# Attention's routing parts of VectorE placed by a table of steps

## The chip, the cores and the metric

One core of one Trainium2 chip runs the whole program as one launch. The metric is the device time of that launch in microseconds (us). A profiled execution of the kernel before comes with its trace.

## What is computed

The input is x, 32 batches of 256 tokens of width 256, with a context of the same shape and a mask of 256x256 for each batch. The reference, cut to what matters:

```python
x = x + cross_attention(layernorm(x), ctx, ctx, mask, Wq, Wk, Wv, Wo, heads=16)   # head width 64
t = layernorm(x)
scores = sigmoid(t @ gate_w.T)                     # 16 experts
_, idx = top_k(scores + gate_b, 4)
w = take(scores, idx); w = w / sum(w) * 2.5
y = sum over the 4 chosen experts e of w_e * (silu_and_mul(t @ w13_e.T) @ w2_e.T)
out = x + y + silu_and_mul(t @ w13_s.T) @ w2_s.T   # one shared expert
```

## The kernel before, in words

The program has two phases. Attention (`emit_attention`) does the 32 batches one after another, 16 heads each, and writes x plus attention to memory; beside it, it already does the routing for the mixture of experts. The expert phase (`expert_phase`) then runs sorted tiles of tokens through the experts. This text is about the attention phase.

**Steps.** A step g is one head: g = 16 b + h, with batch b and h from 0 to 15, 512 steps in all, and a few more at the end. Every engine has its own loop over the steps, written out by hand, and the engines meet by semaphores. In a step TensorE does the scores of head g into `pS` (L888, L889), one projection for a later head into `pj` (a K part in even steps, a Q part in odd ones, L85 to L87, the first "fill"), the transposes of step g-3 into `pT` (L899), in most steps a second fill of `pj` (V at h = 4, 5, 12, 13; a part of Wo at h = 14, 0, 6, 8; transposes at h = 9 and 2; the logits at h = 7), and the values of step g-4 into `pV` (L912). `pj` is two banks: a fill waits until VectorE has emptied the bank of the fill before the last (`bank`, which waits for `s_pjfree`).

**VectorE's step** is, in this order: the masked scores of head g with their maximum, which writes `E` (L1130, two instructions), the inverse sums (L1105), the sum of the two heads' values (L1140), the low part of the first fill (`qk_sp`, L1097), the low part of the transposed probabilities (`PT_lo`, L1149), the low part or sum of the second fill (V L1093, L1078, L1085, L1088), now and then a part of a layer norm (statistics at h = 0, 2, 10, 11; aggregates at h = 4, 12; the norm at h = 6, 8), and last the routing's parts. GpSimd scales `E` by the inverse sums (L792), forms `att_lo` (L741) in even steps, splits the next context at h = 3 (L734, L736), and scatters rows to the experts' order by indirect DMAs (L771).

**Routing.** Two things are done on VectorE in small parts, each part at the end of a step.

- A *choice* (`Router.choose`, part k) takes a set of two batches: sigmoid, bias, the four best of 16 experts, their one-hot rows, their sum as a mask, and the weights. Set s starts at step `SET_FROM[s]` + 1, which is h = 9 of an odd batch, and does one part in each of 15 steps: 0 to 6 at h = 9 to 15, 7 to 14 at h = 0 to 7 of the even batch that follows. Part 11 has two instructions, a product of one-hot rows and scores into `r_prod` (L253) and a sum over it (L256). There are 15 such sets in this phase; a sixteenth is done in the expert phase.
- The *places* (`Router.place`) are computed for two groups of batches, after TensorE has counted ranks (`ranks`) at steps 266 and 426 (h = 10 of batches 16 and 26). Parts 0 to 7 are small. Then come 7 pieces (5 for the second group), each a product into `r_prod` (L327) and a sum (L331), and three parts of `row_of_place`. Before the change they took 18 (16) steps in a row, 267 to 284 and 427 to 442.

The scatters of a group, 8 for a batch and one every 1.5 steps, begin on GpSimd one step after the last part of its places (`scatter_at`), and each batch's rows are loaded again 8 steps before its first scatter (`reload_at`, SP's queue).

Of the kernel before, what the change touches and what calls it, by code (L numbers as in the profile page):

```python
# [41 lines left out]
EARLY_GROUPS = 2  # L42
# [3 lines left out]
SET_BATCHES = 2  # L46
SET_TILES = SET_BATCHES * BATCH_TILES
SETS = GROUP_START[-1] // SET_BATCHES
# [115 lines left out]
class Router:  # L164
# [49 lines left out]
        sc = self.sc[s % 2]  # L214
        act.activation(sc[:, :, :], sc[:, :, :], ACT.Exp, scale=-1.0).then_inc(self.s_exp, 1)

    SET_STEPS = 15

    def choose(self, dve, s, k):
        sc = self.sc[s % 2]  # L220
        at = slice(self.region(SET_TILES * s), self.region(SET_TILES * s) + SET_TILES)
        onehot = self.onehot[:, at, :, :]
        if k == 0:
            dve.wait_ge(self.s_exp, s + 1)
            self.chain(dve.tensor_scalar(sc[:, :, :], sc[:, :, :], 1.0, None, ALU.add))
            return
        self.chain_here(dve)
        if k == 1:
            self.chain(dve.reciprocal(sc[:, :, :], sc[:, :, :]))
        elif k == 2:  # L230
            self.chain(dve.tensor_tensor(self.bi[:, :, :], sc[:, :, :],
                                         self.shared.gate_b[:, :].unsqueeze(1).broadcast_to([P, SET_TILES, N_EXPERTS]), ALU.add))
        elif k in (3, 4):
            for t in range(2 * (k - 3), 2 * (k - 2)):
                last = dve.max(self.top[:, t, :], self.bi[:, t, :])
            self.chain(last)
        elif k in (5, 6):
            for t in range(2 * (k - 5), 2 * (k - 4)):
                last = dve.max_index(self.topi[:, t, :], self.top[:, t, :], self.bi[:, t, :])
            self.chain(last)  # L240
        elif k == 7:
            self.chain(dve.tensor_copy(self.topf[:, :, :], self.topi[:, :, 0:TOPK]))
        elif k == 8:
            self.chain(dve.tensor_tensor(
                onehot, self.shared.iota[:, :].unsqueeze(1).unsqueeze(1).broadcast_to([P, SET_TILES, TOPK, N_EXPERTS]),
                self.topf[:, :, :].unsqueeze(3).broadcast_to([P, SET_TILES, TOPK, N_EXPERTS]), ALU.is_equal))
        elif k == 9:
            self.chain(dve.tensor_tensor(self.halves[:, :, :, :], onehot[:, :, 0:2, :], onehot[:, :, 2:4, :], ALU.add))
        elif k == 10:
            dve.tensor_tensor(self.mask[:, at, :], self.halves[:, :, 0, :], self.halves[:, :, 1, :], ALU.add).then_inc(  # L250
                self.s_mask, 1)
        elif k == 11:
            self.chain(dve.tensor_tensor(self.prod[:, :, :, :], onehot,  # L253
                                         sc[:, :, :].unsqueeze(2).broadcast_to([P, SET_TILES, TOPK, N_EXPERTS]), ALU.mult))
            self.chain_here(dve)
            self.chain(dve.reduce_sum(self.taken[:, :, :], self.prod[:, :, :, :], AXX))  # L256
        elif k == 12:
            self.chain(dve.reduce_sum(self.wsum[:, :], self.taken[:, :, :], AXX))
        elif k == 13:
            self.chain(dve.reciprocal(self.wrec[:, :], self.wsum[:, :]))  # L260
        else:
            dve.scalar_tensor_tensor(self.shared.weight[:, SET_TILES * s:SET_TILES * (s + 1), :], self.taken[:, :, :], ROUTE_SCALE,
                                     self.wrec[:, :].unsqueeze(2).broadcast_to([P, SET_TILES, TOPK]), ALU.mult,
                                     ALU.mult).then_inc(self.s_weight, 1)
# [99 lines left out]
def emit_attention(nc, shared, ident_dram, gate_wT, gate_b, iota, x, ctxT, mask, wqT, wkT, wvT, woT, x2, w13_sT, w2_sT, w13T, w2T):  # L364
# [3 lines left out]
    H = INNER // DH  # L368
# [23 lines left out]
    router = shared.router  # L392
    SET_FROM = [(SET_BATCHES * s + SET_BATCHES + 1) * H + LG_STEP + 1 for s in range(SETS - 1)]
    RANK_STEP = 10
    RANKS_AT = [(GROUP_START[g + 1] + 2) * H + RANK_STEP for g in range(EARLY_GROUPS)]
    SCATTER_STEPS = 1.5
    scatter_at, step = {}, 0.0
    for b in range(GROUP_START[EARLY_GROUPS]):
        g = sum(b >= start for start in GROUP_START[1:GROUPS])
        step = max(step, RANKS_AT[g] + 1 + router.place_steps(g))  # L400
        if step + SCATTER_STEPS * BATCH_TILES * TOPK >= G:
            break
        for n in range(BATCH_TILES * TOPK):
            scatter_at[int(step)] = (b, n // TOPK, n % TOPK)
            step += SCATTER_STEPS
# [10 lines left out]
    with ExitStack() as ctx:  # L416
# [607 lines left out]
        def _(dve):  # L1024
# [93 lines left out]
            for g in steps:  # L1118
# [53 lines left out]
                if g == SHARED_STEP + 1:  # L1172
# [1 line left out]
                    for at, source in ((slice(0, 2 * EXPERT_WIDTH), c_in.tiles[0]), (slice(2 * EXPERT_WIDTH, None), shared.gate)):  # L1174
                        dve.tensor_tensor(shared.sw13[1][:, :, at], source[:, :, :], f32(shared.sw13[0][:, :, at]), ALU.subtract)
                    dve.tensor_tensor(shared.sw2[1], c_in.tiles[1][:, 0, :], f32(shared.sw2[0]), ALU.subtract).then_inc(shared.s_swlo, 1)
                for t, start in enumerate(SET_FROM):
                    if start < g <= start + router.SET_STEPS:
                        router.choose(dve, t, g - start - 1)
                for c in range(EARLY_GROUPS):  # L1180
                    if RANKS_AT[c] < g <= RANKS_AT[c] + router.place_steps(c):
                        if g == RANKS_AT[c] + 1:
                            dve.wait_ge(s_pjfree, number[("rk", c)] + 1)
                        router.place(dve, c, g - RANKS_AT[c] - 1)


def count_of(kind, units):
# [768 lines left out]
```

## Time and profile before

| what | value |
|---|---|
| median of 3 runs | 2213.93 us |
| lowest and highest | 2211.66 and 2216.16 us |
| the profiled execution's own time | 2211.4 us |
| its span | 2209.6 us |
| busy: PE, DVE, ACT, POOL | 94%, 84%, 76%, 63% |
| granted TensorE clock, mean | 0.988 |

The span is the time between the first and the last recorded instruction. PE is TensorE's matmuls, DVE is VectorE, ACT is ScalarE, POOL is GpSimd, SP is the engine whose queue starts the plain DMAs. Matmuls are pipelined, so their durations overlap, and so do those of VectorE's instructions a little: what one of them costs its queue is the distance from its start to the next one's start. L12 is line 12 of the kernel before. In the changed kernel the lines from 397 on are 12 higher.

### The profile page before, as it was taken

What the parts mean: (1) busy time and instruction counts of PE and PEld (TensorE: products, weight loads), DVE (VectorE), ACT (ScalarE), POOL (GpSimd) and SP (SyncE); (2) the same over time, 40 slices, a digit from 0 to 9 for tenths busy, and PEclk for the clock granted to TensorE, in tenths of its full rate; (3) what the DMA queues carried; (4) which work ended last, traced back from release to release, by engine and by line L of the source; (5) the groups of instructions that cost most, each with busy time, mean ns of one, the idle gap of its engine ahead of it and who ended that gap; (6) DMA issues with size and microseconds to landing.
All of it is one profiled execution on the core that took longest, in us unless ns stands there. A gap on an engine that the chain in (4) does not pass through costs nothing. (4 is left out here: it accounts for less than half of the span.)

```text
span 2209.6 us, 57976 instructions
## 1 busy us (share of the span) xinstructions
PE 2086.8 (94%) x16512; PEld 2006.3 (91%) x16512; DVE 1865.4 (84%) x6129; ACT 1677.5 (76%) x4795; POOL 1400.1 (63%) x2094
## 2 busy tenths in 40 slices
PE   7999999999999999999999999999899998898885
PEld 6999999999999998999999998999799998888884
DVE  7999999999999999999999999999764446666687
ACT  6989889888888888898898888889655554454531
POOL 4555655555555555888778877876656646656665
PEclk9999999999999999999999999999999999999997
DMA  7777767777777766866666666666678768887897
GB/s 207 188 182 191 187 175 187 184 181 192 179 187 184 182 168 169 220 188 171 176 180 174 176 167 162 177 172 167 217 254 277 266 240 283 274 283 269 268 331 242
DMA packets 262128, 457.32 MB, mean 207 GB/s; under 512 B 36544, under 2 KB 148672, under 8 KB 261824
## 3 DMA queue, kind: packets, MB, share of 16 engines
q1 hardware_dynamic: 237248, 386.48, 62.8%
q0 software_dynamic: 24576, 67.14, 9.5%
q8 instruction: 148, 2.42, 0.4%
q14 instruction: 156, 1.28, 0.2%
HBM read 141.00 MB, written 144.70 MB: 129 GB/s over the span
## 5 line engine op out<-in xcount | busy, mean ns | idle before, releaser
L792 POOL TENSOR_SCALAR E<-E,rinv 128x256 f32<-128x256 f32 x1024 | 479.6, 479 | 474.8 <-DVE rinv L1105 470.0
L980 ACT ACTIVATE E<-E,negmax 128x256 f32<-128x256 f32 x1024 | 508.9, 502 | 6.8 <-DVE negmax L1130 6.6
L1130 DVE CUSTOM_DVE_ANT_0 E<-pS,m_in 128x256 f32<-128x256 f32 x1024 | 387.5, 416 | 34.4 <-PE pS L889 30.9
L1149 DVE TENSOR_TENSOR PT_lo<-pT,PT_hi 128x512 fp32r<-128x512 f32 x512 | 350.6, 685 | 27.7 <-ACT PT_hi L998 23.6
L1602 POOL DMA_INDIRECT block<-expert_rows,slot x256 | 247.0, 965 | 168.5 <-remote 69.9
L998 ACT ACTIVATE PT_hi<-pT 128x512 fp32r<-128x512 f32 x512 | 304.9, 596 | 9.7 <-PE pT L899 0.5
L899 PE MATMUL pT<-ident,E 128*128 128x128 f32 x2048 | 306.6, 272 | 0.4 <-POOL E L792 0.4
L912 PE MATMUL pV<-PT_hi,V 128*128 128x256 f32 x1024 | 287.2, 303 | 6.1 <-DVE PT_lo L1149 6.0
L964 ACT ACTIVATE qk_sp<-pj 128x256 fp32r<-128x256 f32 x512 | 196.4, 384 | 109.1 <-PE pj L87 95.7
L888 PE MATMUL pS<-qk_st 128*128 128x256 f32 x1024 | 269.1, 284 | 7.8 <-DMA qk_st<-qk_sp 7.6
L889 PE MATMUL pS<-qk_st,qk_sp 128*128 128x256 f32 x1024 | 266.4, 282 | 0.0
L912 PE MATMUL pV<-PT_lo,V 128*128 128x256 f32 x1024 | 265.4, 281 | 0.0
L899 PEld LDWEIGHTS pT<-ident,E 128*128 128x128 f32 x2048 | 235.9, 141 | 0.8 <-POOL E L792 0.6
L1097 DVE TENSOR_TENSOR qk_sp<-pj,qk_sp 128x256 fp32r<-128x256 f32 x512 | 215.0, 420 | 10.6 <-ACT qk_sp L964 2.7
L1140 DVE TENSOR_TENSOR att_sum<-pV,att_sum 64x256 f32<-64x256 f32 x512 | 211.4, 413 | 11.2 <-ACT att_sum L989 1.9
L741 POOL TENSOR_TENSOR att_lo<-att_sum,att_hi 128x256 fp32r<-128x256 f32 x256 | 192.4, 751 | 24.2 <-ACT att_hi L1007 20.5
L912 PEld LDWEIGHTS pV<-PT_hi,V 128*128 128x128 f32 x1024 | 193.9, 189 | 14.3 <-DVE PT_lo L1149 8.6
L989 ACT ACTIVATE att_sum<-pV 64x256 f32<-64x256 f32 x512 | 193.8, 379 | 16.4 <-PE pV L912 4.1
L888 PEld LDWEIGHTS pS<-qk_st 128*128 128x128 f32 x1024 | 195.5, 191 | 10.1 <-DMA qk_st<-qk_sp 9.8
L912 PEld LDWEIGHTS pV<-PT_lo,V 128*128 128x128 f32 x1024 | 194.6, 190 | 6.1
L980 ACT ACTIVATION_READ_ACCUMULATOR E<-E,negmax 128x1 f32 x1024 | 197.9, 193 | 0.0
L889 PEld LDWEIGHTS pS<-qk_st,qk_sp 128*128 128x128 f32 x1024 | 195.7, 191 | 0.1
(265 smaller groups left out, 6879.3 us busy)
## 6 DMA issues: line engine op xcount, KB each, us to landing
qk_st<-qk_sp SPq DMA_DIRECT2D x512, 192.0 KB
qk_st<-qk_sp SPq DMA_DIRECT2D x512, 128.0 KB
sorted_rows<-qk_st SPq DMA_DIRECT2D x152, 256.0 KB, 3.5
xg<-sorted_rows SPq DMA_DIRECT2D x76, 512.0 KB
expert_rows<-block SPq DMA_DIRECT2D x76, 512.0 KB
acc<-x_plus_attention SPq DMA_DIRECT2D x35, 256.0 KB
x_in<-in_x SPq DMA_DIRECT2D x32, 256.0 KB
c_in<-in_ctxT SPq DMA_DIRECT2D x32, 256.0 KB, 4.0
```

Source lines behind the costliest of these rows:

```text
L792: last = pool.tensor_scalar(e[:, t, :], e[:, t, :], rinv[:, r, t:t + 1], 1.0, ALU.mult, ALU.mult)
L888: pe.matmul(pS[g % 2][:, t, :], stacked[:, a, Q_HI, at], stacked[:, a, K_HI, :], start=True, stop=False)
L889: last = pe.matmul(pS[g % 2][:, t, :], plain[:, Q_HI, at], stacked[:, a, K_LO, :], start=False, stop=True)
L899: last = pe.transpose(pT[g % 2][:, k, t * P:(t + 1) * P], e[:, t, k * P:(k + 1) * P], ident[:, :])
L912: last = pe.matmul(pV[g % 2][:, 0:S], V[:, k, j, 2 * a:2 * a + 2, :], PT[g % PT_RING][part][:, k, :], start=k + part == 0, stop=k == NT - ...
L980: last = act.activation(E[r][:, t, :], E[r][:, t, :], ACT.Exp, bias=negmax[:, r, t:t + 1], scale=-1.0, accum_out=rowsum[:, r, t:t + 1])
L998: act.activation(PT[m % PT_RING][0][:, :, :], pT[m % 2][:, :, :], ACT.Copy).then_inc(s_pthi, 1)
L1097: last = dve.tensor_tensor(plain[:, lo, :], ps[:, 0:S], f32(plain[:, hi, :]), ALU.subtract)
L1130: last = dve.tensor_tensor_reduce(out=E[r][:, t, :], in0=pS[g % 2][:, t, :], in1=m_in.tile(b)[:, t, :], scale=-1.0, scalar=BIG, op0=ALU.ad ...
L1140: dve.tensor_tensor(att_sum[pair % 2][half(a), :], pV[n % 2][half(a), 0:S], att_sum[pair % 2][half(a), :], ALU.add).then_inc(s_sum, 1)
L1149: dve.tensor_tensor(lo[:, :, :], pT[n % 2][:, :, :], f32(hi[:, :, :]), ALU.subtract).then_inc(s_ptlo, 1)
L1602: pool.indirect_dma_start(out=cbuf[n % NCB][:, j, :], out_offset=None, in_=expert_rows[g], in_offset=bass.IndirectOffsetOnAxis(ap=shared.s ...
```

## The change

A table `CHOICE_AT` says at which offset from h = 0 of the odd batch each part of a choice is done, in place of one part a step. Part 11's two instructions become parts 11 and 12, and the later parts are renumbered, so a choice has 16 parts. The new places: parts 0, 1, 2 at h = 9, 10, 11 as before; 3 and 4 at h = 13 and 14; 5 and 6 together at h = 15; 7 and 8 together at h = 1 of the even batch; the product (11) at h = 3, ahead of the mask's parts 9 and 10 at h = 5 and 6; the sum and the weights' parts at h = 7 (12, 13) and h = 8 (14, 15). Nothing of a choice is left at h = 12, 0, 2 and 4. The places keep one part a step for offsets 1 to 9, then follow `QUIET_STEPS`: offsets 11, 13, 15, 16, 17, 19, 20, 21, 23. Batch 17's h = 4, 6, 8 and 12 become free of them, and the last part of the first group comes at step 289 in place of 284, of the second group at 446 in place of 442. A choice that would overlap with places is moved by a whole batch: set 7 starts at step 297 in place of 281, set 12 at 457 in place of 441. The scatters follow the places: the first is at step 290 in place of 285, the last at 504 in place of 499.

```diff
-    SET_STEPS = 15
+    SET_STEPS = 16
...
         elif k == 11:
             self.chain(dve.tensor_tensor(self.prod[:, :, :, :], onehot,
                                          sc[:, :, :].unsqueeze(2).broadcast_to([P, SET_TILES, TOPK, N_EXPERTS]), ALU.mult))
-            self.chain_here(dve)
+        elif k == 12:
             self.chain(dve.reduce_sum(self.taken[:, :, :], self.prod[:, :, :, :], AXX))
-        elif k == 12:
+        elif k == 13:
             self.chain(dve.reduce_sum(self.wsum[:, :], self.taken[:, :, :], AXX))
-        elif k == 13:
+        elif k == 14:
             self.chain(dve.reciprocal(self.wrec[:, :], self.wsum[:, :]))
...
     RANKS_AT = [(GROUP_START[g + 1] + 2) * H + RANK_STEP for g in range(EARLY_GROUPS)]
+    CHOICE_AT = {9: (0,), 10: (1,), 11: (2,), 13: (3,), 14: (4,), 15: (5, 6), 17: (7, 8), 19: (11,), 21: (9,), 22: (10,), 23: (12, 13), 24: (14, 15)}
+    QUIET_STEPS = (9, 11, 13, 15, 16, 17, 19, 20, 21, 23)
+
+    def place_offsets(c):
+        return [*range(1, router.PLACE_STEPS + 1), *QUIET_STEPS][:router.place_steps(c)]
+
+    def choice_start(s):
+        at = (SET_BATCHES * s + SET_BATCHES + 1) * H
+        crowded = any(at + min(CHOICE_AT) <= RANKS_AT[c] + place_offsets(c)[-1] and RANKS_AT[c] < at + max(CHOICE_AT)
+                      for c in range(EARLY_GROUPS))
+        return at + H if crowded else at
+
...
-        step = max(step, RANKS_AT[g] + 1 + router.place_steps(g))
+        step = max(step, RANKS_AT[g] + 1 + place_offsets(g)[-1])
...
-                for t, start in enumerate(SET_FROM):
-                    if start < g <= start + router.SET_STEPS:
-                        router.choose(dve, t, g - start - 1)
+                for t in range(SETS - 1):
+                    for k in CHOICE_AT.get(g - choice_start(t), ()):
+                        router.choose(dve, t, k)
                 for c in range(EARLY_GROUPS):
-                    if RANKS_AT[c] < g <= RANKS_AT[c] + router.place_steps(c):
+                    if g - RANKS_AT[c] in place_offsets(c):
                         if g == RANKS_AT[c] + 1:
                             dve.wait_ge(s_pjfree, number[("rk", c)] + 1)
-                        router.place(dve, c, g - RANKS_AT[c] - 1)
+                        router.place(dve, c, place_offsets(c).index(g - RANKS_AT[c]))
```

Two places in VectorE's order show it. The first is a choice at h = 4 of batch 4, the even batch of set 0. `E4` and `E3` are the masked scores that open a step, `V` is the second fill's low part, `mv` the layer norm's aggregate. Before:

```order
L1097 TENSOR_TENSOR qk_sp0<-pj0,qk_sp0 128x256
L1149 TENSOR_TENSOR PT2_lo<-pT1,PT2_hi 128x512
L1093 TENSOR_TENSOR V<-pj1,V 128x4x128
L1035 BN_AGGR mv<-st6 128x2 x2
L253 TENSOR_TENSOR r_prod<-r_onehot,r_sc0 128x256
L256 TENSOR_REDUCE r_taken<-r_prod 128x16
L1130 ISA E4,negmax<-pS1,m_in0 128x256
```

In the changed kernel, the end of h = 3 of that batch, and the end of its h = 4:

```order
L1152 TENSOR_TENSOR att_sum1<-pV0,att_sum1 64x256
L1109 TENSOR_TENSOR qk_sp2<-pj1,qk_sp2 128x256
L1161 TENSOR_TENSOR PT1_lo<-pT0,PT1_hi 128x512
L253 TENSOR_TENSOR r_prod<-r_onehot,r_sc0 128x256
L1142 ISA E3,negmax<-pS0,m_in0 128x256
```

```order
L1109 TENSOR_TENSOR qk_sp0<-pj0,qk_sp0 128x256
L1161 TENSOR_TENSOR PT2_lo<-pT1,PT2_hi 128x512
L1105 TENSOR_TENSOR V<-pj1,V 128x4x128
L1047 BN_AGGR mv<-st6 128x2 x2
L1142 ISA E4,negmax<-pS1,m_in0 128x256
```

The product has moved one step ahead, from behind `V` and the aggregate to behind `PT_lo` of a step without a second fill, and the sum has left this stretch (it now closes h = 7).

The second place is the first group's places in batch 17, at the end of h = 4. Before:

```order
L1149 TENSOR_TENSOR PT0_lo<-pT1,PT0_hi 128x512
L1093 TENSOR_TENSOR V<-pj1,V 128x4x128
L1035 BN_AGGR mv<-st6 128x2 x2
L327 TENSOR_TENSOR r_prod<-r_onehot,r_pos 128x256
L331 TENSOR_REDUCE r_places<-r_prod 128x16
L1130 ISA E2,negmax<-pS1,m_in1 128x256
```

In the changed kernel, the same stretch, and the end of h = 5:

```order
L1109 TENSOR_TENSOR qk_sp2<-pj0,qk_sp2 128x256
L1161 TENSOR_TENSOR PT0_lo<-pT1,PT0_hi 128x512
L1105 TENSOR_TENSOR V<-pj1,V 128x4x128
L1047 BN_AGGR mv<-st6 128x2 x2
L1142 ISA E2,negmax<-pS1,m_in1 128x256
```

```order
L1161 TENSOR_TENSOR PT1_lo<-pT0,PT1_hi 128x512
L1105 TENSOR_TENSOR V<-pj1,V 128x4x128
L327 TENSOR_TENSOR r_prod<-r_onehot,r_pos 128x256
L331 TENSOR_REDUCE r_places<-r_prod 128x16
L1142 ISA E3,negmax<-pS0,m_in1 128x256
```

The piece that closed h = 4 now closes h = 5. TensorE's and ScalarE's orders are untouched. On GpSimd the scatters, and on SP the reloads of rows, come five steps later.

## Rows read from the trace of the kernel before

**Rows 1.** The page: span; busy us, share of the span, instructions.
```profile
span 2209.6 us, 57976 instructions
PE 2086.8 (94%) x16512; PEld 2006.3 (91%) x16512; DVE 1865.4 (84%) x6129; ACT 1677.5 (76%) x4795; POOL 1400.1 (63%) x2094
```

**Rows 2.** TensorE's waits from 19 to 1566 us: waiter, what for, us, times, longest.
```profile
PE pj L85 <- DVE qk_sp L1097: 12.9, 28, 0.9
PE pV L912 <- DVE PT_lo L1149: 6.0, 7, 1.4
```

Of a window the columns are: from and to, its length, then busy us (instructions) of PE, of PE's weight loads, of DVE, ACT and POOL, the granted clock (1.00 is full), the DMA engines' share and GB/s.

**Rows 3.** Windows of batches 2, 4, 5, 17, 18, 27, cut at TensorE's scores.
```profile
112.91:159.68 46.77, 46.77 (x378) 45.68 (x377) 43.03 (x150) 41.88 (x127) 26.88 (x49) 1.00 0.74 187
206.93:254.50 47.57, 47.26 (x378) 45.82 (x377) 44.85 (x163) 42.28 (x127) 27.13 (x49) 1.00 0.74 184
254.50:301.75 47.25, 47.07 (x375) 45.48 (x374) 43.95 (x160) 41.87 (x127) 26.33 (x48) 1.00 0.73 185
...
827.57:880.74 53.17, 49.26 (x379) 46.32 (x377) 51.85 (x190) 43.47 (x128) 26.71 (x48) 1.00 0.67 169
880.74:930.35 49.61, 47.93 (x378) 45.99 (x377) 46.48 (x163) 42.70 (x127) 39.46 (x61) 1.00 0.81 214
...
1312.39:1366.92 54.53, 49.60 (x378) 46.32 (x377) 53.13 (x186) 43.61 (x128) 39.09 (x59) 1.00 0.58 158
```

**Rows 4.** Windows of single steps: h = 3 and 6 of batch 2; h = 3, 5, 6 of batch 4.
```profile
121.12:123.22 2.10, 2.10 (x21) 2.10 (x19) 2.10 (x7) 2.08 (x8) 1.10 (x2) 1.00 0.90 234
...
130.23:133.77 3.54, 3.54 (x33) 3.54 (x32) 3.25 (x11) 3.49 (x12) 2.58 (x6) 1.00 0.76 190
215.11:217.41 2.30, 2.30 (x20) 2.16 (x19) 2.27 (x7) 2.25 (x9) 1.44 (x3) 1.00 0.81 183
...
220.92:224.43 3.51, 3.51 (x27) 3.24 (x26) 3.48 (x10) 3.14 (x10) 3.05 (x4) 1.00 0.86 218
224.43:228.59 4.16, 3.85 (x33) 3.64 (x32) 4.10 (x16) 3.40 (x11) 2.95 (x7) 1.00 0.50 122
```

**Rows 5.** TensorE's timeline in batch 4: h = 5 begins, and h = 6's first fill.
```profile
220.92 0.28 PE L888 MATMUL pS<-qk_st 128*128 128x256 f32 x1
...
225.37 0.39 PE L85 MATMUL pj<-cT_hi,wk_hi 128*128 128x256 f32 x1 [0.31 <-DVE qk_sp L1097]
```

**Rows 6.** VectorE's timeline in batch 4: start and end of h = 4, start of h = 5.
```profile
219.31 0.41 DVE L1130 CUSTOM_DVE_ANT_0 E<-pS,m_in 128x256 f32<-128x256 f32 x1
...
222.33 1.13 DVE L253 TENSOR_TENSOR r_prod<-r_onehot,r_sc 128x256 f32<-128x256 bf16 x1
...
223.83 0.42 DVE L1130 CUSTOM_DVE_ANT_0 E<-pS,m_in 128x256 f32<-128x256 f32 x1
```

**Rows 7.** GpSimd's timeline in batch 4, around h = 3 and 4 of VectorE.
```profile
218.21 0.93 POOL L792 TENSOR_SCALAR E<-E,rinv 128x256 f32<-128x256 f32 x2 [1.44 <-DVE rinv L1105]
...
221.89 1.29 POOL L736 TENSOR_TENSOR cT_lo<-c_in,cT_hi 128x512 fp32r<-128x512 f32 x1
```

**Rows 8.** VectorE's timeline in batch 17: the piece at h = 3, then h = 4 begins.
```profile
840.26 0.41 DVE L327 TENSOR_TENSOR r_prod<-r_onehot,r_pos 128x256 f32<-128x256 bf16 x1
840.70 0.42 DVE L331 TENSOR_REDUCE r_places<-r_prod 128x16 f32<-128x256 f32 x1
841.04 0.41 DVE L1130 CUSTOM_DVE_ANT_0 E<-pS,m_in 128x256 f32<-128x256 f32 x1
```

**Rows 9.** Windows of h = 4 and h = 5 of batch 17.
```profile
838.07:841.77 3.70, 3.70 (x26) 3.25 (x25) 3.67 (x16) 3.43 (x10) 0.93 (x2) 1.00 0.86 244
841.77:846.03 4.26, 3.82 (x27) 3.33 (x26) 4.16 (x14) 3.26 (x10) 3.66 (x5) 1.00 0.72 179
```

**Rows 10.** VectorE's timeline at h = 15 of batch 3: one part of two searches.
```profile
207.89 0.08 DVE L239 MATCH_VALUE_LOAD r_topi<-r_top,r_bi 128x8 f32 x1
...
208.19 0.41 DVE L1130 CUSTOM_DVE_ANT_0 E<-pS,m_in 128x256 f32<-128x256 f32 x1
```

**Rows 11.** The instructions that read `r_topi`: duration in ns, min/median/max.
```profile
L242 DVE CAST r_topf<-r_topi x16: 155/158/775, 211.1 to 1606.2; 128x16 f32<-128x16 uint32 x16
```

## Prediction

> **What bounds the kernel.** The page comes first: TensorE is busy 94% of the span, VectorE 84% [rows 1]. So a step lasts as long as TensorE's work in it, unless TensorE waits. Its waits over the attention phase are few, and nearly all are for VectorE: 12.9 us in 28 waits for `qk_sp`, which frees the bank of `pj` for the next fill, and 6.0 us in 7 for `PT_lo` [rows 2]. Next, windows cut at batches, which all hold the same 375 to 379 matmuls at full clock [rows 3]. Batch 2, which has no part of a choice yet, takes 46.77 us with TensorE never idle: that is the floor. Batches 4 and 5, the even and the odd half of an ordinary choice, take 47.57 and 47.25, 0.80 and 0.48 more. Batch 17, with the first group's places, takes 53.17, batch 18 49.61 and batch 27, with the second group's, 54.53. In 17 and 27 VectorE is busy 51.85 and 53.13 us, over 97%: there it sets the pace, as nowhere else.
>
> **How lateness becomes time.** I call VectorE's *lateness* at a step the time from TensorE's first scores of the step (L888) to VectorE's first scores of it (L1130). The first fill of a step that follows a step with two fills waits for `qk_sp` of that step, which VectorE reaches a fixed time after its scores. So the loss is lateness minus that step's length plus a constant. In batch 4 the lateness at h = 5 is 223.83 - 220.92 = 2.91 us, the step 3.51, and h = 6 takes 4.16 in place of 3.54 [rows 4 to 6]: 0.62 lost, a constant of 1.22. Its wait stands in the trace, 0.31 idle, and the rest is weights loaded late [rows 5]. For the other parity, batch 17: lateness 841.04 - 838.07 = 2.97 at h = 4, a step of 3.70, and h = 5 takes 4.26 in place of 3.51 [rows 4, 8, 9]: 0.75 lost, a constant of 1.48.
>
> **An ordinary choice, 12 of them** (sets 0 to 6, 8 to 11, 13). The 0.80 of the even batch is 0.62 at h = 6 and 0.20 at h = 3 (2.30 against 2.10) [rows 4].
> - *h = 4 loses product and sum.* They cost VectorE 223.83 - 222.33 = 1.50 us [rows 6]. The product alone, put at h = 3, should cost what the same instruction in the places does there, 840.70 - 840.26 = 0.44 [rows 8], while the mask's small part leaves that step. The lateness at h = 5 so goes from 2.91 to about 1.8, against 2.3 (3.51 - 1.22) from which h = 6 loses anything. The 0.62 goes.
> - *Why the product costs 1.13 at h = 4* [rows 6] *and 0.41 at h = 3* [rows 8]: at h = 4 it begins at 222.33, inside GpSimd's 1.29 us split of the context (221.89 to 223.18), and ends 0.28 after it [rows 7]. The split waits for GpSimd's scaling of step 3, which needs VectorE's inverse sums of step 4, so it cannot come before the end of h = 3. The Trainium skill (SBUF — State Buffer, "Who interferes with whom") says that VectorE and GpSimd share a port pair as an exclusive lock, and that a VectorE tensor_tensor with both inputs in SBUF waits for a GpSimd instruction that reads SBUF. For the split of the context the trace agrees.
> - *h = 15 gets a second part of two searches*, 208.19 - 207.89 = 0.30 us [rows 10], and h = 1 the cast beside the one-hot part, some 0.1 (its 0.16 overlapped [rows 11]). Step h = 0 loses that cast. All of it comes before h = 3, the step that already loses 0.20. Between nothing and 0.40 of it gets through. VectorE still waits on others for parts of h = 15, 0 and 1, so I take 0.12: the loss at h = 3 becomes about 0.32.
> - *h = 5 to 8* get parts of 0.1 to 0.5 us. Lateness is then small, so 0. At h = 5 itself the product of h = 3 counts. The lateness at h = 4 was 219.31 - 217.41 = 1.90 [rows 4, 6]; with the product for the mask's part (0.1), the 0.12 of above, and TensorE's own 0.12 lost at h = 3, it is about 1.90 + 0.34 + 0.12 - 0.12 = 2.2 at the most and 2.0 if VectorE's idle time absorbs a part. The loss is that - 3.51 + 1.48, so 0 to 0.2, right at the point where it begins; I take 0.
> - *The odd batch* keeps its parts at h = 9 to 11, from which its 0.48 comes. The part that leaves h = 12 is behind `qk_sp` of that step: 0.
>
> Net 0.62 - 0.12 = 0.50 per choice, 12 x 0.50 = **6.0 us**. Bounds: 0.22 (all 0.40 gets through) to 0.80 (no loss left), 2.6 to 9.6.
>
> **The places and the two moved choices.** Where VectorE sets the pace, what leaves it is gained one for one. From batch 17: the first seven parts of set 7, worth at least 43.95 - 43.03 = 0.9 busy us by batches 5 and 2 [rows 3], up to 1.6 where no idle time absorbs them; the collision at h = 4, 0.7; and the last part of the rows, about 0.5, which goes to batch 18, where lateness can be paid back. That is 2.1 to 2.8 us, and going free at h = 4, 6, 8, 12 lets TensorE run without a wait at h = 6 to 9; I take 3.0. The piece at h = 3 stays, and with it the 0.75 lost at h = 5. Batch 18 loses the second half of a choice (0.8) and gets the spill from the last parts, net 0.5 gained. Batch 27: as batch 17, but all parts of the rows stay in it: 1.6 to 2.4, with fewer collisions perhaps 3.2; I take 3.1. Batches 19, 28 and 29 exchange half choices: set 12 leaves batch 28 (0.8, of which the new first half takes 0.5), and the second halves that arrive in odd batches cost 0.3 each: -0.3 together. Batch 16 and 26 keep ranks and parts 0 to 4. In all 3.0 + 0.5 + 3.1 - 0.3 = **6.3 us**. Bounds: 3.4, if only the certain work counts, to 15, if all three batches fall to the 47.4 of an ordinary one: (53.17 + 49.61 + 54.53) - 3 x 47.4.
>
> **The rest.** Scatters come five steps later in the same queue at the same spacing, and still end at step 504, before the phase does; the reloads likewise: 0. Ranks wait for the mask, now at h = 6 of the even batch in place of h = 3; TensorE asks for it at h = 10: 0. At the end of the phase the cast of set 14, 0.775 us long somewhere against a median of 0.158 [rows 11], moves by a step: 0 to 0.6 gained, I take 0.5 with the sixteenth set's shift of one unit at 0. The expert phase starts earlier by what is gained and is otherwise as it was.
>
> **Sum.** 6.0 + 6.3 + 0.5 = 12.8 us, 0.6%. Against the profiled execution's own 2211.4 that is 2198.6; the median of the runs is 2.5 higher, so **2201.1 us** for the median. Bounds 2.6 + 3.4 to 9.6 + 15 + 0.6: a gain of 6 to 25.
>
> **Rivals.**
> - *Almost all lateness goes.* Spreading clears `qk_sp` everywhere, and the gain is near 22: 2192. For: TensorE's waits for VectorE are 18.9 us in all [rows 2]. Against: the parts at h = 9 to 11, at h = 3 and the ranks stay. 0.07.
> - *The pace in 17 and 27 stays VectorE's.* Only work that leaves counts: 6.0 + 3.4 = 9.4, so 2204.5. 0.12.
> - *The product collides at h = 3 too.* GpSimd's scaling of `E`, two instructions of 0.48, ends at 219.14, just before the end of VectorE's h = 3 [rows 7]. If the product falls into it and waits 0.5, then lateness at h = 4 is 2.5, and h = 5 loses 0.5 by the rule above, in 14 pairs: 12.8 - 7.0 = 5.8, so 2208. Against: in batch 17 the piece at that place took 0.41. By the same section of the Trainium skill the scaling reads SBUF and would block the product if it started first. 0.08.
> - *The doubled parts cost more than the emptied ones give: slower.* Place: h = 15 and h = 1, ahead of h = 3. It decides once what it costs passes 0.62 in each of 14 pairs, and the 6.3 of the places on top: 1.07 per pair. If the cast at h = 1 takes 0.775 in place of 0.158, adds to the 0.40, and reaches h = 3 and then h = 5 in full, that is 2.0 lost against 0.62 won: 14 x 1.4 = 20 us lost, less the 6.3 of the places: 2227. Against: `r_topf` is at 0.158 in the median. 0.02.
> - *No net change:* the scatters' and reloads' new steps, or DMAs that VectorE's new order starts at other times, bring waits of their own and take back what is won: 2213. Against: batch 18, the only one here with scatters and no places, is late by 2.8 us, of which a choice explains 0.8. 0.03.
>
> **Numbers.** The forecast has 0.68. A measurement of this kernel can tell about 0.2%, 4.4 us, from no change. Faster by more than that: 0.68 + 0.07 + 0.12 and half of the collision's 0.08 and more, 0.92. Within it 0.06, slower 0.02. The range 2193 to 2208 takes in the second rival and most of the bounds, and leaves out the floor's extreme, the slower case and no change.
>
> **What would show it.** In the profile after: h = 6 of even batches at 3.5 with no wait for `qk_sp`; L253 at 0.41 in the median, not 1.13; ordinary even batches near 47.1; batch 17 near 50 and batch 27 near 51.5, with VectorE under 97% busy; waits for `qk_sp` down from 28 to some 12. The forecast is wrong if h = 3 or h = 5 of even batches grows by over 0.3, if L253 stays over 1 us, or if batches 17 and 27 stay over 52.

## The result, and the profile after

The changed kernel took 2203.95 us in the median of 6 runs (2196.77 to 2207.86), the kernel before 2213.07 beside it (6 runs, 2208.03 to 2216.16): a ratio of 0.9954, 95% interval 0.9935 to 0.9974. By the ratio that is 10.2 us less, 5.8 to 14.4 by its interval. The forecast was 12.8 less. Two runs of later kernels, 3356.26 us at a mean granted clock of 0.56 (*places_only*) and 2857.81 us at 0.65 (*reload_9*), are in no ratio below.

The profiled execution of the changed kernel is the slowest of its six, 2207.86 us. Its page (span; then busy us, share, instructions, as in [rows 1]):

```profile
span 2206.0 us, 57976 instructions
PE 2083.2 (94%) x16512; PEld 2008.8 (91%) x16512; DVE 1857.1 (84%) x6129; ACT 1676.6 (76%) x4795; POOL 1402.9 (64%) x2094
```

So this execution is only 3.6 us shorter than that of [rows 1]. TensorE's waits in the attention phase (19 to 1566 us; waiter, what for, us, times, longest) say what stands against the gain:

```profile
PE pS L900 <- DMA qk_st<-qk_sp: 10.1, 10, 2.7
PE pj L85 <- DVE qk_sp L1109: 6.9, 20, 0.7
PE pV L924 <- DVE PT_lo L1161: 5.0, 6, 1.5
```

Waits for VectorE's `qk_sp` went from 12.9 us in 28 [rows 2] to 6.9 in 20. Waits of the scores for a copy of the queries, which SP's queue moves (`qk_st<-qk_sp`), went from 4.0 us in 6 to 10.1 in 10.

The batches, cut at TensorE's first scores, in the changed kernel: batches 4, 5, 17, 18, 19, 27 (columns as in [rows 3]):

```profile
208.52:255.68 47.16, 47.02 (x379) 45.73 (x377) 44.70 (x167) 42.08 (x127) 27.06 (x49) 1.00 0.74 185
255.68:302.92 47.24, 47.06 (x378) 45.77 (x377) 43.86 (x157) 42.15 (x128) 26.84 (x49) 1.00 0.74 185
827.29:877.38 50.09, 48.30 (x378) 46.04 (x377) 48.16 (x168) 43.26 (x128) 26.20 (x48) 1.00 0.72 177
877.38:927.33 49.95, 47.80 (x378) 45.92 (x377) 46.55 (x168) 42.55 (x127) 36.47 (x58) 1.00 0.80 204
927.33:979.48 52.15, 49.14 (x378) 47.35 (x377) 46.39 (x174) 42.54 (x128) 37.69 (x58) 0.97 0.66 173
1312.21:1363.66 51.45, 48.48 (x379) 46.02 (x378) 49.53 (x174) 43.38 (x128) 39.83 (x60) 1.00 0.61 162
```

Against [rows 3]: batch 4 from 47.57 to 47.16, 17 from 53.17 to 50.09, 27 from 54.53 to 51.45, and VectorE in both no longer over 97% busy but 96%. Batch 19, 47.59 before, is 4.6 us longer, at a mean clock of 0.97. Batch 5 can't be compared as it stands in [rows 3]: that window ends at 301.75, 0.43 us before the first scores of batch 6 at 302.18, and so holds 375 matmuls. To those scores it is 47.68, with a wait for a copy in it; the other ordinary odd batches of the kernel before took 47.21 to 47.25.

Steps h = 2 to 6 of batch 4 (in the same columns):

```profile
214.16:216.71 2.55, 2.55 (x24) 2.55 (x23) 2.48 (x11) 2.50 (x9) 0.94 (x3) 1.00 0.68 188
216.71:219.22 2.51, 2.37 (x21) 2.16 (x19) 2.48 (x8) 2.46 (x9) 1.66 (x3) 1.00 0.73 165
219.22:222.72 3.50, 3.50 (x26) 3.23 (x25) 3.44 (x16) 3.11 (x10) 1.44 (x4) 1.00 0.94 270
222.72:226.23 3.51, 3.51 (x26) 3.24 (x25) 3.51 (x13) 3.14 (x10) 3.42 (x6) 1.00 0.97 227
226.23:229.76 3.53, 3.53 (x32) 3.53 (x31) 3.24 (x12) 3.48 (x12) 2.85 (x7) 1.00 0.76 189
```

h = 6 is back at 3.53 from 4.16 [rows 4]; h = 3 has grown from 2.30 to 2.51. The product's row (duration in ns, min/median/max), in the changed kernel:

```profile
L253 DVE TENSOR_TENSOR r_prod<-r_onehot,r_sc x16: 405/406/411, 220.9 to 1608.0; 128x256 f32<-128x256 bf16 x16
```

All 16 take 0.41 us. At h = 4 it had been 1.13 in batch 4 [rows 6], and that is also the median of the 16 before. The end of VectorE's h = 1 of batch 4 (start, duration):

```profile
215.14 0.16 DVE L242 CAST r_topf<-r_topi 128x16 f32<-128x16 uint32 x1
215.33 0.42 DVE L244 TENSOR_TENSOR r_onehot<-iota,r_topf 128x256 bf16<-128x256 f32 x1
215.68 0.42 DVE L1142 CUSTOM_DVE_ANT_0 E<-pS,m_in 128x256 f32<-128x256 f32 x1
```

The cast now costs its queue 215.33 - 215.14 = 0.19 us here.

**Batch 19.** TensorE's timeline at the end of its h = 5 (start, duration; in brackets the idle time before and what ended it), then two windows:

```profile
944.93 0.28 PE L924 MATMUL pV<-PT_lo,V 128*128 128x256 f32 x1
947.95 0.58 PE L900 MATMUL pS<-qk_st 128*128 128x256 f32 x1 [2.74 <-DMA qk_st<-qk_sp]
```

```profile
944.00:947.70 3.70, 1.21 (x8) 0.87 (x6) 2.31 (x5) 2.41 (x7) 3.52 (x6) 1.00 0.92 214
947.70:951.10 3.40, 3.15 (x15) 3.15 (x16) 1.47 (x7) 0.39 (x1) 2.67 (x4) 0.50 0.47 121
```

TensorE stood idle for 2.74 us, and 0.28 us before it went on the granted clock fell to 0.50 for 3.4 us, the lower of its two levels (1.2 GHz). Matmuls of 0.28 us took 0.41 in that time, and the first one 0.58. Wait and clock together make the two steps 6.41 and 5.06 us long in place of 3.51 and 3.53: 4.4 us. SP's queue before it:

```profile
936.56 0.60 SPq L656 DMA_DIRECT2D sorted_rows<-qk_st  x1
937.21 0.62 SPq L615 DMA_DIRECT2D c_in<-in_ctxT  x1
937.87 1.18 SPq L623 DMA_DIRECT2D m_in<-in_mask  x1
939.15 0.39 SPq L667 DMA_DIRECT2D sv<-xn_rows  x1
939.64 0.49 SPq L642 DMA_DIRECT2D qk_st<-qk_sp  x1
```

The copies are queued behind four other transfers, one of them the reload `sv`, which the change has moved to here. In the kernel before the copies for the same step stand behind three:

```profile
938.97 0.99 SPq L644 DMA_DIRECT2D sorted_rows<-qk_st  x1
940.01 0.93 SPq L603 DMA_DIRECT2D c_in<-in_ctxT  x1
940.98 1.00 SPq L611 DMA_DIRECT2D m_in<-in_mask  x1
942.09 0.48 SPq L630 DMA_DIRECT2D qk_st<-qk_sp  x1
```

### The profile page after: what moved, and what is told of

Read it like the earlier page. It is cut to its first block and busy times, and to the rows that moved or that the text cites. A ratio compares the mean times of both kernels' runs of the same rounds, so it can differ in the third digit from the quotient of the medians.

```text
span 2206.0 us, 57976 instructions
## 1 busy us (share of the span) xinstructions
PE 2083.2 (94%) x16512; PEld 2008.8 (91%) x16512; DVE 1857.1 (84%) x6129; ACT 1676.6 (76%) x4795; POOL 1402.9 (64%) x2094
## 5 line engine op out<-in xcount | busy, mean ns | idle before, releaser
L1152 DVE TENSOR_TENSOR att_sum<-pV,att_sum 64x256 f32<-64x256 f32 x512 | 211.4, 413 | 11.2 <-ACT att_sum L1001 1.7
```

Of the source, the lines that this page charges most:

```text
L1152: dve.tensor_tensor(att_sum[pair % 2][half(a), :], pV[n % 2][half(a), 0:S], att_sum[pair % 2][half(a), :], ALU.add).then_inc(s_sum, 1)
```

## The experiments

The kernels were timed in five groups, each with runs of the kernel before beside them, so ratios are compared, not times. The kernel before had medians of 2213.07 us (beside the result), 2201.99 (experiments 1 to 4), 2125.21 (5 to 8), 2209.76 (9) and 2125.44 (10). Windows, waits and latenesses are of one profiled execution of each kernel.

**1. again.** The changed kernel, unaltered.

> The changed kernel once more, on one chip with the three runs beside it. Lateness theory: batch windows repeat to 0.1 us where only VectorE and TensorE meet (batch 4 at 47.16, batch 17 at 50.1, batch 27 at 51.45), and the gain is 9 to 13 us. Two theories for batch 19, which took 52.15 with TensorE 2.74 us idle on the copy of qk_sp and a slow clock behind it: (a) the reload of rows, now one step after the context's and the mask's loads while the clearing still runs, holds the copy up, so it comes back at the same step in every execution; (b) transfers jitter from one execution to the next, so it is absent or elsewhere here, and batch 19 takes about 47.8.

0.9946 (0.9933 to 0.9959; 2191.07 against 2201.99). Batches 17 and 27: 50.08 and 51.41. Batch 19: 49.19, with a wait of 0.98 us at the same step. The forecast windows repeat to 0.05 us; the wait comes again at the same step, as theory (a) had it, but shorter and with no fall of the clock.

**2. choice_only.** The choices as in the change; places in a row as before, no set moved, scatters where they were.

```diff
-        return [*range(1, router.PLACE_STEPS + 1), *QUIET_STEPS][:router.place_steps(c)]
+        return [*range(1, router.place_steps(c) + 1)]
...
-        return at + H if crowded else at
+        return at
```

> Only the choices follow the table; the places keep one part a step, no set is moved, scatters and reloads as before. Lateness theory: 0.4 us less in each even batch (47.16 for 47.57), batches 17 and 27 within 0.8 us of before but for the product's collision in even batch 18: 5 to 6.5 us gained. Theory that the places carry the whole gain: under 2 us.

0.9976 (0.9966 to 0.9985): 5.3 us. Its windows of batches 4, 17, 27:

```profile
207.28:254.43 47.15, 47.00 (x378) 45.71 (x377) 44.69 (x167) 42.07 (x127) 27.05 (x49) 1.00 0.74 185
824.76:877.90 53.14, 49.25 (x379) 46.30 (x377) 51.77 (x186) 43.51 (x128) 27.07 (x48) 1.00 0.68 170
1306.29:1360.75 54.46, 49.62 (x378) 46.30 (x377) 52.78 (x182) 43.64 (x128) 39.27 (x59) 1.00 0.59 158
```

Batch 4 has all its gain, 17 and 27 none. Batch 19 took 47.57, with no wait for a copy at h = 6.

**3. places_only.** Places, moved sets and scatters as in the change; the choice one part a step, product and sum at h = 4.

```diff
-    CHOICE_AT = {9: (0,), 10: (1,), 11: (2,), 13: (3,), ...}
+    CHOICE_AT = {9 + n: (k,) for n, k in enumerate(range(11))} | {20: (11, 12), 21: (13,), 22: (14,), 23: (15,)}
```

> Only the places follow the quiet steps, sets 7 and 12 are moved and the scatters come five steps later; a choice does one part a step with product and sum together at h = 4, as before. Lateness theory: batch 17 at 50.1 and batch 27 at 51.5, ordinary even batches at 47.57: 5 to 7 us gained if nothing stalls, 4 less where batch 19 stalls on the copy. If (a) holds for the stall it is here too.

0.9973 (0.9961 to 0.9985): 5.9 us. Batches 4, 17, 27:

```profile
207.78:255.34 47.56, 47.24 (x378) 45.80 (x377) 44.85 (x163) 42.30 (x127) 27.16 (x49) 1.00 0.74 184
829.35:879.44 50.09, 48.20 (x379) 46.07 (x377) 48.14 (x168) 43.21 (x128) 26.10 (x48) 1.00 0.72 178
1311.01:1362.22 51.21, 48.38 (x379) 46.09 (x377) 49.58 (x174) 43.37 (x128) 39.16 (x60) 1.00 0.62 163
```

The mirror image. 5.3 and 5.9 make 11.2, against 11.9 for both in the same group: the two halves add. Batch 19 waited 0.57 us for the copy at h = 6.

**4. reload_9.** The reloads one step earlier.

```diff
-    reload_at = {step - 8: b for step, (b, t, j) in scatter_at.items() if t + j == 0}
+    reload_at = {step - 9: b for step, (b, t, j) in scatter_at.items() if t + j == 0}
```

> The changed kernel with each batch's rows loaded 9 steps before its first scatter in place of 8, which puts the reloads back at h = 5, 1, 13, 9 as before the change. Theory (a), the reload behind the context's loads makes batch 19's stall: batch 19 takes 47.7 and the whole is 4 us faster than the changed kernel. Theory (b), jitter: no difference in the median, and stalls on the copy elsewhere in the profile.

0.9955 (0.9942 to 0.9968), no better than *again*. Batch 19 had no wait at h = 6 in this execution (48.45 us), but batch 20 had one of 0.54 at h = 12. The edit does less than was expected of it. The reload that stands in batch 19 does not go back to where it was (in the kernel before it is issued before that batch begins). It only changes places in the same queue, from behind the context and the mask to ahead of them, and there are still four transfers ahead of the copies.

**5. product_h4.** The changed kernel with part 11 alone moved back (`20: (11,)` for `19: (11,)`); one execution.

> The changed kernel with one move undone: the product (L253) is back at h = 4 of the even batch, alone, its sum still at h = 7. Port theory: it takes 1.13 us again in 12 or more of 16 cases, as it meets GpSimd's split of the context. Lateness theory: that alone costs nothing much, since lateness at h = 5 comes to about 2.3, the point where h = 6 begins to lose: h = 3 at 2.5 or 0.1 less, h = 6 at 3.53 to 3.65, even batches at 47.15 to 47.3. Rival, that the collision as such was the old loss: h = 6 back at 4.1 and even batches at 47.6.

2117.59 us beside 2125.21. L253's row in it:

```profile
L253 DVE TENSOR_TENSOR r_prod<-r_onehot,r_sc x16: 392/1132/1353, 222.6 to 1603.7; 128x256 f32<-128x256 bf16 x16
```

The product alone, without its sum, is back at 1.13, so it is the place and not the pair that makes it dear. But its price alone costs next to nothing at h = 6. The windows of h = 6 of batch 4, here and in *floor_choice* (experiment 9):

```profile
224.92:228.45 3.53, 3.53 (x32) 3.53 (x31) 3.47 (x12) 3.29 (x11) 2.70 (x7) 1.00 0.59 143
223.40:227.15 3.75, 3.75 (x32) 3.62 (x31) 3.69 (x13) 3.01 (x10) 2.89 (x6) 1.00 0.46 108
```

The lateness at h = 5 was 2.23 here, just under the 2.29 from which h = 6 loses, and 2.50 there. Over the ten ordinary even batches (4 to 14, 20 to 24 and 30) h = 6 took 3.59 in the mean here, 4.17 in the kernel before and 3.53 in *again_2*. So what else the table changes ahead of h = 6, the sum gone from h = 4 and the mask's part from h = 3, gave 0.58 of the 0.64, and moving the product the last 0.06. These ten batches gain 0.7 us together, against 3.3 in *again_2*, but of the 2.6 between them only 0.6 is at h = 6; the rest is at h = 5, 8, 11 and 12 of single batches. Eight stand between 47.15 and 47.57, batch 30 at 48.02 and batch 24 at 48.63.

**6. split_search.** `14: (4, 5), 15: (6,)` for `14: (4,), 15: (5, 6)`; one execution.

> The changed kernel with the first part of the searches at h = 14 beside part 4, the second alone at h = 15. If the pair of searches at h = 15 is what raised the loss at h = 3 from 0.20 to 0.41: h = 3 at 2.3 and even batches at 46.95. If it is the cast at h = 1: h = 3 stays at 2.45 or more.

2114.71 us. Lateness at h = 0 fell from 1.69 to 1.27 us and at h = 1 from 1.08 to 0.68, but at h = 2 it stayed at 1.51, and h = 3 at 2.51. The second search of h = 15 is therefore not what lengthens h = 3: a wait of VectorE's in h = 1 takes it in. What stands between is the rest of h = 1, where the cast now sits ahead of the one-hot part. The timelines show both. In the kernel before VectorE waits 0.23 us for `PT_hi` in h = 1 of batch 4 and begins `PT_lo` 2.46 us after TensorE's first scores; in the changed kernel it does not wait and begins it at 2.49, and from there the 0.19 of the cast is nearly all that is new (lateness at h = 2 rose by 0.21).

**7. slack_choice.** A table that keeps h = 9 to 11, 15 and 1 to 4 free: `{12: (0,), 13: (1,), 14: (2, 3, 4), 16: (5,), 21: (6, 7), 22: (8, 9, 10), 23: (11, 12), 24: (13, 14, 15)}`.

> The changed kernel with another table for the choices: parts only in steps in which TensorE's own work is longer than VectorE's (h = 12, 13, 14, 0, 5, 6, 7, 8), none at h = 9, 10, 11, 15, 1, 2, 3, which are VectorE's light steps but TensorE's short ones. Lateness theory: no loss at h = 3 nor at h = 13, even and odd batches both at the floor of 46.8, so 0.4 less in each of some 26 batches: 10 us faster than the changed kernel, ratio to the kernel before 0.990. Rival, that VectorE's total load matters and not the place: no change against the changed kernel, 0.9946.

0.9966 (0.9955 to 0.9978), far from the 0.990 expected. Ten ordinary odd batches (3 to 15, 21 to 25) gained 4.4 us, and eight of them stand at the floor, 46.75 to 46.77; the ten even ones lost 3.4, most of it after scatters have begun (batch 20: 49.05). In batch 24 VectorE's one-hot part, then what GpSimd did at that time:

```profile
1184.04 1.00 DVE L244 TENSOR_TENSOR r_onehot<-iota,r_topf 128x256 bf16<-128x256 f32 x1
```

```profile
1184.01 0.75 POOL L753 TENSOR_TENSOR att_lo<-att_sum,att_hi 128x256 fp32r<-128x256 f32 x1
```

The scatter ahead of it (1.10 us on GpSimd) has pushed `att_lo` to where VectorE's part runs; before the scatters the same part takes 0.42.

**8. slack_all.** As 7, and the places given the steps with the most slack as well, several small parts to a step; a scatter every 1.45 steps, reloads 9 steps ahead.

> As slack_choice, and the places put by the same rule (offsets 1 to 4, 6, 11 to 13, 18 to 20, 27 to 30, for the second group 27 to 29), scatters from step 297 every 1.45 steps, reloads 9 steps ahead. Lateness theory: batch 17 at 47 to 48, batch 18 at 48, batch 27 at 47 to 48: another 6 to 7 us, ratio to before 0.987. Rival, that VectorE is the bound in those batches: batch 17 stays over 49.5.

0.9955 (0.9942 to 0.9968), against 0.987 expected. Batch 17 fell to 48.22 and 27 to 48.82, 10.7 us off both together, where the rival had 17 stay over 49.5; batch 18 rose to 52.75, with waits of 1.76 and 1.81 us for the queries' copies and a fall of the clock, and the waits for such copies came to 12.1 us in all.

**9. again_2 and floor_choice**, in one group. The second is a table from what 5 to 7 showed: `{12: (0,), 13: (1,), 14: (2, 3, 4), 16: (5,), 19: (6,), 20: (7,), 21: (8,), 22: (9, 10), 23: (11, 12), 24: (13, 14, 15)}`, reloads 9 steps ahead, the rest as in the change.

> The changed kernel unaltered, a third time, as the neighbour of the next run. Both theories: 0.9950 of the kernel before, between 0.993 and 0.997. Theory A (the wait of batch 19 belongs to the shifted scatters with their reload 8 steps ahead): a TensorE wait of 0.5 to 3 us for the queries' copy at h = 6 of batch 19. Theory B (such waits wander): none there, and others elsewhere. The even batch's h = 3 takes 2.50, its h = 6 3.53.

> A table made from what the runs showed. Odd batch: nothing at h = 9 to 11, parts 0, 1 and 2 to 4 at h = 12, 13, 14. Even batch: one search at h = 0, the other at h = 3, the cast at h = 4, the one-hot at h = 5, both mask parts at h = 6, product and sum at h = 7, the rest at h = 8. Places, moved choices and scatters as in the change, reloads one step earlier. By lateness: odd batches 46.8 (they lost 0.48 at h = 12 and 13), even ones 46.8 to 46.9 (h = 3 back at 2.10; h = 4 reaches 2.0 with one search, just under 2.03, from which h = 5 loses). 12 choices x (0.48 + 0.40) = 10.6 us less than the changed kernel at the most; since scatters slow whatever overlaps them and the batches 16 to 18 and 26 to 28 hardly change, I take 6 to 8: 0.9915 of the kernel before. Rival 1: the one-hot at h = 5 or the product at h = 7 falls beside a GpSimd instruction and takes 0.9 us in place of 0.43: even batches at 47.3 to 48, and the gain of the odd ones is lost again: 0.995. Rival 2: what TensorE no longer waits for, it waits for at other places of its own chain (clock dips, copies of queries): batches at the floor and yet no faster than the changed kernel.

*again_2*: 2201.47 (2200.20 to 2203.32), 0.9966 (0.9952 to 0.9979), a wait of 1.49 us at h = 6 of batch 19, as theory A had it. *floor_choice*: 2196.75 (2194.65 to 2197.82), 0.9941 (0.9927 to 0.9954). It is 4.7 us under the changed kernel beside it, and their runs do not overlap: the best version of this study, and less than the 6 to 8 expected. Its cast at h = 4 meets the same split as the product had (next).

**10. floor_again and cast_h5**, in one group: the same table, and one with `21: (7, 8)` for `20: (7,), 21: (8,)`.

> The table of floor_choice a second time, as neighbour of the next run: 0.994 of the kernel before. The cast at h = 4 of the even batch takes 0.88 us beside GpSimd's split of the context, as in floor_choice, and batches 4 and 6 take 0.2 to 0.5 more than the floor at h = 5 and 6.

> floor_choice with its one collision taken out: the cast (L242) goes from h = 4 to h = 5, ahead of the one-hot. Theory: cast at 0.16 us in place of 0.88, lateness at h = 5 down from 2.5 to about 1.2 and at h = 6 near 1.5; h = 5 and 6 at 3.51 and 3.53 in all even batches, h = 10 at 2.10 before the scatters. Gain over floor_choice 12 x 0.1 to 0.35 = 1 to 4 us of attention: 0.9925 of the kernel before. Rival: the cast or the one-hot then falls beside GpSimd's E scaling or rowsum work at h = 5 and takes as long there: no gain, 0.994. Rival 2: the attention phase is 1 to 4 us shorter and the time does not follow, because the waits for the queries' copies at h = 12 grow by as much.

In *floor_again*, 0.9929 (0.9915 to 0.9943), the cast of 16 numbers a partition sits beside GpSimd's split of the context. VectorE's row, then GpSimd's:

```profile
222.45 0.88 DVE L242 CAST r_topf<-r_topi 128x16 f32<-128x16 uint32 x1
```

```profile
222.01 1.29 POOL L748 TENSOR_TENSOR cT_lo<-c_in,cT_hi 128x512 fp32r<-128x512 f32 x1
```

In *cast_h5* it is out of there. Its row of the cast, and batches 4 and 19:

```profile
L242 DVE CAST r_topf<-r_topi x16: 164/176/394, 225.3 to 1599.7; 128x16 f32<-128x16 uint32 x16
```

```profile
206.97:253.75 46.78, 46.78 (x379) 45.69 (x377) 44.82 (x168) 42.15 (x127) 27.23 (x50) 1.00 0.75 187
924.40:977.14 52.74, 49.42 (x378) 47.45 (x377) 47.54 (x174) 42.83 (x128) 37.84 (x59) 0.97 0.65 171
```

An even batch with its half choice at the floor, every step as in batch 2: the best VectorE can do for TensorE. Yet the kernel is not faster: 2113.36 against 2109.90 in the same group, 0.9943 (0.9929 to 0.9956), with ranges that overlap. Batch 19 waits 2.95 us for the copy, at the very reload distance that had shown none in *reload_9*, and the copies' waits are 11.9 us in 14, against 5.4 in 9 for *floor_again*. So of the second rival the waits for copies grew, those at h = 12 from 2.5 to 5.2 us among them, but its other half did not come: from the first scores to the last this execution is 11.5 us longer than that of *floor_again*, not 1 to 4 shorter. It is also the slowest of its five, 6.9 us over their median. How much of this the median holds is not shown.

## Why the prediction was right, and where not

Changes of each batch's length against the kernel before, in us, one profiled execution each (from TensorE's first scores of the batches; "even" is ten ordinary even batches, 4 to 14, 20 to 24 and 30):

| | even | 16, 26 | 17 | 18 | 27 | 19 | 28, 29 |
|---|---|---|---|---|---|---|---|
| after | -3.5 | -0.9 | -3.1 | +0.3 | -3.1 | +4.6 | +0.3 |
| again | -2.1 | -0.9 | -3.1 | -0.5 | -3.1 | +1.6 | +0.9 |
| again_2 | -3.3 | -0.9 | -3.1 | -0.9 | -3.1 | +2.2 | +0.3 |
| choice_only | -3.8 | -0.9 | 0.0 | -1.6 | -0.1 | 0.0 | +0.8 |
| places_only | +1.0 | 0.0 | -3.1 | -0.7 | -3.3 | +0.7 | +0.6 |

- **Where lateness becomes time: right.** The law with its two constants, read from batches 4 and 17, holds in the changed kernel without a new number. With 1.51 at h = 5 nothing is lost at h = 6, as 2.3 was the limit. *product_h4* and *floor_choice* test that limit from both sides: 2.23 loses nothing (3.53), and 2.50 should lose 2.50 - 3.51 + 1.22 = 0.21 and loses 0.22 (3.75). It holds also where I did not apply it: at h = 3, loss = lateness at h = 2 - 2.55 + 1.48, which gives 0.23 for the 1.30 before (measured 0.20), 0.44 for the 1.51 after (0.41), and nothing for the 0.97 of *slack_choice* (2.10, nothing). In the thirteen executions other than that of the kernel before, batches 2 to 30, it gives a loss of over 0.03 us at h = 3, 5 or 6 in 194 cases, and in 191 of them the measured one is within 0.06.
- **The product's price: right.** 1.13 at h = 4 (median) and 0.41 at h = 3, forecast from another instruction of the same shape in batch 17. The feared collision at h = 3 came in none of the 16. The Trainium skill's rule on the shared port pair (SBUF — State Buffer, "Who interferes with whom") agrees with the trace again where the one-hot part met GpSimd's `att_lo`: 1.00 in place of 0.42 us.
- **An ordinary choice: 0.50 forecast, 0.42 found** (47.57 to 47.16), 12 x 0.42 = 5.0 for 6.0; *choice_only* measured 5.3 on the whole, the sets 7 and 12 included (batch 18 alone is 1.6 shorter in its profile). The 0.62 at h = 6 went as forecast (lateness at h = 5 came to 1.51 where I had put 1.8), but by *product_h4* nearly all of it came with the sum's leaving h = 4 and the mask's part leaving h = 3, not with the end of the collision. The term mis-sized is the growth of h = 3, put at 0.12 and found at 0.21, and its cause as well. The prediction charged it to the searches at h = 15 with a small share for the cast. *split_search* showed the reverse: the searches vanish in VectorE's waits, and the cast ahead of the one-hot costs 0.19 at h = 1, one for one. Lateness at h = 2 rose by 0.21, and by the law above the loss with it. Applying the law at h = 3 as at h = 6 would have given the number. The 0.20 feared at h = 5 did not come (lateness at h = 4 was 2.0, as taken). The 0.48 of the odd half was read from a window of batch 5 that ends too early; the other odd batches give the same number, so nothing rests on the slip.
- **Batches 17 and 27: right.** 3.0 and 3.1 forecast. Batch 17 lost 3.1 in every execution with these places. Batch 27 lost 3.1 in the three of the changed kernel and 3.0 to 4.1 in the others. In batch 17 it came where it was forecast: h = 5 still took 4.25, h = 6 to 8 gave 1.3 us, the rest came from h = 10 on. Both sizes were picks from ranges that reached from 2.1 to 2.8 and from 1.6 to 3.2, so that they fit to 0.1 is in part luck. Batch 18, forecast at -0.5, had -0.5 and -0.9 in the two repeats and +0.3 in the profile first taken, which has a wait for a copy in it. Batch 28 fell by 0.5 in two of three for 0.3 forecast, and batch 29 grew by 0.8 for 0.3. *places_only* gave 5.9 us for the forecast 6.3.
- **"The scatters and the reloads: 0" is the step that failed.** Seven executions of kernels with the shifted scatters and the reload 8 steps ahead were profiled: five waited 0.57 to 2.74 us at h = 6 of batch 19, *slack_choice* waited 1.04 at its h = 4, and *product_h4* not at all. Neither *choice_only* nor the kernel before had such a wait in that batch. I gave this mechanism 0.03 as a rival that takes everything back; as a price beside the gain, the wait and what followed it made h = 5 and 6 of batch 19 longer by 4.4, 1.2 and 1.7 us in the three executions of the changed kernel, and the first of them lost more than half of its difference to it. The exact cause stays open. With reloads 9 steps ahead there was no wait at h = 6 of batch 19 in two executions, 0.2 and 0.3 us in two others, and 2.95 in a fifth (*cast_h5*). So the reload's distance is not the whole of it. In eleven executions the reload stands among four transfers just ahead of the copies for h = 6, and seven of these waited there. In the kernel before, in *choice_only* and in *slack_all* it does not stand there, and they waited nothing, nothing and 0.2. But the wait of *slack_choice* at h = 4 ended before its reload was issued, so such waits also come without it ahead of the copies. A run that keeps the shifted scatters and takes the reload out of this stretch would tell the two apart, and none was made.
- **The tail: 0.5 forecast.** The part after the last scores differed by +0.2, -9.0 and -1.1 us in the three executions of the changed kernel against the one of the kernel before. The -9.0 is of the group and not of the change: in the same group *choice_only*, *places_only* and *reload_9* have -10.2, -10.7 and -8.0, and the kernel before had a median 11 us lower. Nothing of 0.5 can be read there, from either side.

In sum 12.8 forecast; 0.9954, 0.9946 and 0.9966 measured, which is 10.2, 11.9 and 7.5 us. From the first scores to the last the three executions are 3.4, 6.8 and 9.1 us shorter than that of the kernel before, for 12.3 forecast in this stretch. What is missing is found nearly whole: 1.0 in the choices, 6.2, 4.2 and 1.5 more of waits for copies, and in the first 1.7 at the lower clock and around it. The execution of the kernel before has the shortest waits for copies of all fourteen (4.0 us; the others 4.9 to 12.1), so how much of this the change brings and how much is chance is not shown.

The waits listed as proof came out at 20 for `qk_sp`, not 12. What is left is mostly short ones at h = 3 of the even batches (0.15 to 0.23 us) and those of batches 17, 18 and 27 (up to 0.7).

## What to carry to other kernels

Side work on an engine that is not the bottleneck costs nothing until that engine's lateness passes the length of the bottleneck's step less a constant; read the constant from one step that loses time, apply it to every step, and move parts to where the bottleneck's step is long, not to where the helper has little to do. A small part can cost what it overlaps: look at what GpSimd runs at that moment, since a cast of 16 numbers a partition took 0.88 us beside its split. Yet such a price loses time only above the limit: the product at 1.13 us at h = 4 lost almost nothing by itself, and 0.62 with its sum behind it and a part of the mask one step ahead. When such a move starts transfers at other times, count the queue that carries them as a term of its own, and look at what now stands in it ahead of the copies that the bottleneck waits for.

## What was not expected of the hardware

- After waits of TensorE for a copy of 1.81 us (*slack_all*), 2.74 (the changed kernel) and 2.95 (*cast_h5*) the granted clock was 0.50 for 3.4 us; it fell between 0.3 us before and 0.5 us after the end of the wait. After waits of 0.98, 1.49 and 1.76 it did not fall. The length of the wait alone does not decide: at h = 8 of batch 0 all fourteen executions waited 1.76 to 2.18 us, and the clock fell within 1.5 us behind it in two of them (1.85 in *again*, 2.16 in *product_h4*), but not behind the 2.18 of the changed kernel. The fall raised the price of the 2.74 us wait to some 4.4.
- The waits for the queries' copies wander between executions of one kernel. Batch 2, which the change does not touch, took 46.76, 47.34 and 47.68 us in three executions of the changed kernel; the long two have such a wait at h = 12. Their sum over the phase was 10.1, 8.1 and 5.5 us in these three.
- The same kernel before ran in 2202 to 2213 us in three groups and in 2125 in two. The group medians of 2201.99 and 2209.76 are from one chip, those of 2125.21 and 2125.44 from two others. The kernels profiled in the faster groups have attention phases like the rest (1518 to 1530 us from the first scores to the last, 1520 to 1535 elsewhere), and 570 to 574 us after the last scores, where the others have 646 to 658. The cause is not known.
- VectorE's maxima and searches (0.14 to 0.18 us), the reciprocal of the scores (0.53 to 0.55) and the sums over `r_prod` (0.40 to 0.42) kept their times at every place that the tables gave them. The product (0.39 to 1.49), the one-hot part (0.40 to 1.00), the cast (0.14 to 1.13) and the weights' last part (0.15 to 0.53) did not.
